# One core, a Perceiver layer with a top-2 mixture of experts: the first slot tiles in another order, and a gather that nobody reads

## What is computed

```python
x = x + xattn(layernorm(x), ctx_1024, ...)   # 16 heads, 257 keys per batch
x = x + mix(layernorm(x), WB, WBf, w1, w2, b)
x = x + moe(layernorm(x), gate, w0, w1, wo)

# moe, 8 experts, F = 512, TOPK = 2
weights, selected = top_k(inputs @ gate, 2)
weights = softmax(weights)
layer_1, layer_2 = sorted_hidden @ w0[e], sorted_hidden @ w1[e]
layer_3 = (silu(layer_1) * layer_2) @ wo[e]
out = sum over the two choices of weights * layer_3
```

## Time and profile before

| | |
|---|---|
| median of 3 runs | 232.37 us (231.4 to 232.68) |
| profiled execution, its own time | 230.8 us |
| its span (first to last instruction) | 229.0 us |
| mean granted TensorE clock | 0.984 of full |
| TensorE busy | 211.3 us, 92% of the span |
| VectorE, ScalarE, GpSimd busy | 66%, 62%, 57% |
| chain that ended last | TensorE 79%, DMA 6%, VectorE 6%, GpSimd 3%, "issue" 2% |

### The profile page before, as it was taken

The page is one execution under the profiler, slowest core; times in us unless marked ns, Lnnn a source line. Parts: engine busy times, 40 slices in busy tenths (PEclk is TensorE's granted clock), DMA queues, the critical chain, the costliest instruction groups (busy, mean ns, idle before and its releaser), DMA issues.

```text
span 229.0 us, 6348 instructions
## 1 busy us (share of the span) xinstructions
PE 211.3 (92%) x2123; PEld 176.6 (77%) x2123; DVE 150.3 (66%) x504; ACT 141.0 (62%) x440; POOL 129.9 (57%) x268
## 2 busy tenths in 40 slices
PE   6789999999999999999987887997999999999980
PEld 6567778778777776867864874796999999999870
DVE  2789769778686877858768587933445565555702
ACT  2488897888899888879875446651224444444300
POOL 2665474566647554561526733947777777773312
PEclk9999999999999999999999999799999999999996
DMA  6888134070411910000000004402212211121053
GB/s 182 291 280 306 63 67 168 0 232 0 161 74 27 337 54 3 1 4 0 4 3 0 1 3 116 71 3 47 58 49 46 58 40 51 45 35 35 2 186 93
DMA packets 12817, 18.30 MB, mean 80 GB/s; under 512 B 1903, under 2 KB 8435, under 8 KB 12786
## 3 DMA queue, kind: packets, MB, share of 16 engines
q1 hardware_dynamic: 10946, 14.77, 20.4%
q0 software_dynamic: 1408, 2.58, 5.1%
q10 hardware_dynamic: 432, 0.54, 0.7%
HBM read 14.20 MB, written 4.01 MB: 80 GB/s over the span
## 4 chain that ended last, share of the span: by engine, by line
PE 79%; DMA 6%; DVE 6%; POOL 3%; issue 2%; ACT 1%; POOLq 1%; SPq 0%; DVEq 0%
PE bank L1041 17%; PE bank L845 12%; PE bank L835 10%; PE bank L817 8%; PE bank L877 8%; PE bank L1052 8%; PE bank L819 6%; DMA pt_sb<-planes 2%; PE bank L1010 2%; PE bank L854 2%; DMA vec_sb<-vectors 2%; DMA slot_sb<-table,slot_row 1%; PE bank L1028 1%; DMA planes<-y_sb,y_row 1%; DVE neg_max L1201 1%
## 5 line engine op out<-in xcount | busy, mean ns | idle before, releaser
L669 ACT ACTIVATE p_sb<-bank,neg_max 128x257 f32<-128x257 f32 x128 | 59.1, 475 | 16.0 <-DVE neg_max L1201 16.0
L1201 DVE TENSOR_REDUCE neg_max<-bank 128x1 f32<-128x257 f32 x128 | 46.7, 418 | 6.4 <-PE bank L835 6.0
L678 ACT ACTIVATE pt_sb<-bank 128x512 f32<-128x512 f32 x64 | 35.0, 612 | 0.6 <-PE bank L845 0.6
L508 POOL TENSOR_TENSOR o_half<-o_masked 128x64 f32<-128x64 f32 x32 | 10.2, 320 | 44.1 <-DVE o_masked L1230 44.1
L845 PE MATMUL bank<-ident,p_sb 128*128 128x128 f32 x256 | 33.2, 273 | 0.0
L1041 PE MATMUL bank<-slot_ft,w_now 128*128 128x128 f32 x240 | 30.9, 276 | 0.0
L1041 PEld LDWEIGHTS bank<-slot_ft,w_now 128*128 128x128 f32 x240 | 29.1, 192 | 0.3 <-issue 0.3
L845 PEld LDWEIGHTS bank<-ident,p_sb 128*128 128x128 f32 x256 | 29.0, 141 | 0.3 <-issue 0.3
L745 ACT ACTIVATE slot_ft<-bank 128x128 f32<-128x128 f32 x23 | 6.4, 278 | 35.9 <-PE bank L1028 33.1
L567 POOL DMA_INDIRECT slot_sb<-table,slot_row x23 | 22.8, 991 | 9.6 <-issue 5.8
L587 POOL DMA_INDIRECT planes<-y_sb,y_row x21 | 21.5, 1023 | 11.4 <-DVE y_sb L1472 5.8
(11 more groups left out here) (212 smaller groups left out, 359.0 us busy)
## 6 DMA issues: line engine op xcount, KB each, us to landing
w_sb<-w SPq DMA_DIRECT2D x8, 512.0 KB, 4.8
ctx_sb<-ctx_keys SPq DMA_DIRECT2D x7, 512.0 KB, 4.3
wo_sb<-wo SPq DMA_DIRECT2D x8, 256.0 KB, 5.3
planes<-zero_rows SPq DMA_DIRECT2D x2, 512.0 KB, 6.8
pt_sb<-planes SPq DMA_DIRECT2D x4, 256.0 KB, 4.7
table<-rows_tok SPq DMA_DIRECT2D x4, 195.0 KB
out<-norm_tok SPq DMA_DIRECT2D x2, 256.0 KB, 2.4
x_tok<-x SPq DMA_DIRECT2D x1, 448.0 KB, 4.9
```

What stands on the lines that cost most here:

```text
L669: act.activation(p_sb[b % 2][:, g, :], s_bank[g][:, 0:SKV], ACT.Exp, bias=neg_max[b % 2][:, g:g + 1], accum_out=sum_last[:, 0, b, g:g + 1] ...
L678: act.activation(pt_sb[b % 2][:, t, :], pt_bank[t][:], ACT.Copy).then_inc((pt0_ready, pt1_ready)[t], 1)
L1201: dve.tensor_reduce(neg_max[b % 2][:, g:g + 1], s_bank[g][:, 0:SKV], AX.X, ALU.max, negate=True).then_inc(max_ready, 1)
```

## The change

It has six parts.

1. `keep_sum(1)` moves ahead of the ranks, behind `keep_sum(0)`.
2. Of tile 1's one-hots GpSimd makes one (token tile 0) in place of four; VectorE makes the other three in one instruction, behind `at_slot`. TensorE's products of tile 1 are put in the order token tile 0, tiles 4 to 7, tiles 1 to 3.
3. `name_slots` moves ahead of tile 1's product.
4. `turn_slots(s + 1)` for s = 1 and 2 moves ahead of `project(s - 1)`.
5. GpSimd issues one more indirect DMA ahead of its one-hots: 128 times row 2048 of the table into `slot_sb[5]`. Nobody reads it; its landing is waited for ahead of the real gathers.
6. For that, a column `no_row` that holds 2048, and a semaphore of its own for the storing of the empty row.

```diff
+        no_row = sb("no_row", [128, 1], U32)
...
-            sp.dma_start(table[TABLE_ROWS:TABLE_ROWS + 1, :], empty_row[0:1, :]).then_inc(table_stored, 16)
+            sp.dma_start(table[TABLE_ROWS:TABLE_ROWS + 1, :], empty_row[0:1, :]).then_inc(empty_stored, 16)
...
+                pool.iota(no_row[:], [[0, 1]], base=TABLE_ROWS, channel_multiplier=0).then_inc(consts_ready, 1)
...
+            pool.wait_ge(consts_ready, 13)
+            pool.wait_ge(empty_stored, 16)
+            pool.indirect_dma_start(slot_sb[SLOT_BUFS - 1][:], None, table, bass.IndirectOffsetOnAxis(no_row[:], 0)
+                                    ).then_inc(first_gather_in, 16)
+
             pool.wait_ge(early_rank_ready, 1)
             for s in range(EARLY):
-                for t in range(HT):
+                for t in range(HT if s == 0 else 1):
                     pool.tensor_scalar(late_at[s][:, t, :], far_slot_nos[:], early_rank[:, t, s:s + 1], None, ALU.is_equal
                                        ).then_inc(pool_at_ready[s], 1)
 
-            pool.wait_ge(table_stored, 16 * (TOPK * len(GROUPS) + 1))
+            pool.wait_ge(table_stored, 16 * TOPK * len(GROUPS))
             pool.wait_ge(slot_row_ready, 1)
+            pool.wait_ge(first_gather_in, 16)
             for s in (2, 0, 3, 1, 4, 5):
                 gather(s)
...
             keep_sum(0)
+            keep_sum(1)
             pe.wait_ge(chosen_ready, 1)
...
-            keep_sum(1)
...
+            def early_features_1():
+
+                pe.wait_ge(pool_at_ready[1], 1)
+                early_product(1, 0, True, False)
+                for t in range(HT):
+                    pe.wait_ge(act_at_ready[1], t + 1)
+                    early_product(1, HT + t, False, False)
+                pe.wait_ge(dve_at_ready, 1)
+                for t in range(1, HT):
+                    last = early_product(1, t, False, t == HT - 1)
+                last.then_inc(slot_turned, 1)
...
-            early_features(0)
+            early_features_0()
             half_hidden(0, 0)
             half_hidden(0, 1)
-            early_features(1)
             name_slots()
+            early_features_1()
...
                 half_hidden(s, 1)
+                if s <= EARLY:
+                    turn_slots(s + 1)
                 if s == 1:
                     pe.wait_ge(slot_row_ready, 1)
                 project(s - 1)
-                if s <= EARLY:
-                    turn_slots(s + 1)
...
+            few = [128, HT - 1, 128]
+            dve.tensor_tensor(late_at[1][:, 1:HT, :], far_slot_nos[:].unsqueeze(1).to_broadcast(few),
+                              early_rank[:, 1:HT, 1:2].to_broadcast(few), ALU.is_equal).then_inc(dve_at_ready, 1)
+
             dve.wait_ge(slot_row_done, 1)
```

More of the change, by code:

```diff
@@ L259, in build @@
             sem(n) for n in ("row_in_tile_ready", "at_slot_ready", "slot_row_done", "slot_row_ready"))
+        first_gather_in, empty_stored = sem("first_gather_in"), sem("empty_stored")
         early_rank_ready, apart_ready = (sem(n) for n in ("early_rank_ready", "apart_ready"))
         pool_at_ready, act_at_ready = ([sem(f"{name}{n}") for n in range(EARLY)] for name in ("pool_at_ready", "act_at_ready"))
+        dve_at_ready = sem("dve_at_ready")
         block = stack.enter_context(nc.Block())
@@ L752, in gate_weights @@
                                ACT.Copy).then_inc(gate_w_ready, 1)
-            act.wait_ge(consts_ready, 12)
+            act.wait_ge(consts_ready, 13)
             act.wait_ge(early_rank_ready, 1)
@@ L987, in _ @@
             keep_sum(0)
+            keep_sum(1)
             pe.wait_ge(chosen_ready, 1)
-            pe.wait_ge(consts_ready, 12)
+            pe.wait_ge(consts_ready, 13)
             for t in range(NT):
@@ L1000, in _, with early_product, early_features_0 @@
             last.then_inc(ranks_done, 1)
-            keep_sum(1)
[L1005 to L1011, removed]
+            def early_product(s, t, start, stop):
+                return pe.matmul((bank[3], bank[1])[s][:, 0:128], rows_tok[:, t, 0, 0:D], late_at[s][:, t, :],
+                                 start=start, stop=stop)
+            def early_features_0():
+                for t in range(HT):
+                    pe.wait_ge(pool_at_ready[0], t + 1)
+                    early_product(0, t, t == 0, False)
+                    pe.wait_ge(act_at_ready[0], t + 1)
+                    last = early_product(0, HT + t, False, t == HT - 1)
+                last.then_inc(slot_turned, 1)
+            def early_features_1():
+                pe.wait_ge(pool_at_ready[1], 1)
+                early_product(1, 0, True, False)
+                for t in range(HT):
+                    pe.wait_ge(act_at_ready[1], t + 1)
[3 more added lines that the diff above has]
+                    last = early_product(1, t, False, t == HT - 1)
                 last.then_inc(slot_turned, 1)
@@ L1359, in _ @@
             own(best_at(2))
-            dve.wait_ge(consts_ready, 12)
+            dve.wait_ge(consts_ready, 13)
             te = [128, NT, E]
```

## The result

| | before | changed |
|---|---|---|
| median | 232.4 us (231.4 to 232.68, 4 runs) | 228.28 us (227.94 to 229.48, 4 runs) |
| ratio | 1 | 0.9856, 95% interval 0.9817 to 0.9896 |
| profiled execution, own time | 230.8 us | 227.94 us |
| its span | 229.0 us | 226.1 us |
| mean granted TensorE clock | 0.984 | 0.997 |

The change is faster, by 1.0 to 1.8%. The forecast was 229.3 us, in a range from 227.6 to 231.2.

What follows compares the result with a forecast made beforehand. TensorE, busy 92% of the span, was taken as the bound, with time to win at its slow-clock slice and idle places from 143 to 163 us. 232.37 - 3.1 = 229.3 us; range 227.6 to 231.2.

Steps and rivals of the forecast that it cites:

- The walk along TensorE: TensorE's work followed from 143.35 us at the full clock through half_hidden(4); 3.1 us won in all.
- the signs: Expected in the profile after: earlier half_hidden(0) and slot_row, no idle before turns 2 and 3, clock not below 0.9.
- keep_sum(1), 0.97 us: Moved into TensorE's 0.95 us hole before the ranks at cost 0; half_hidden(0) starts at 147.15, 0.97 us won.
- name_slots and the turns: name_slots first gives slot_row at 149.87, not 152.63; turns ahead of projections start half_hidden(2) at 154.80, not 157.00.
- The spare gather: Extra GpSimd gather before the one-hots, 2.09 us within 3.44 us idle; cost 0, keeps gathers just ahead of TensorE.
- a lag of 0.30 or 0.84 us: First real gather starts 0.84 us after slot_row, or 0.30 if the spare gather takes the first one's extra.
- The bound of 0 to 0.9 us for a late slot 4: At turn 4: without the spare gather's help, slot 4 could hold TensorE by 0 to 0.9 us.
- The last step: From profiled execution to median: 3.1 us taken off 232.37 gives 229.3; the profiled execution was 1.57 us below the median.
- the clock falls elsewhere: Rival, chance 0.37: clock falls during or behind tile 0's product; gain 2.6 us (0.22) or 1.8 us (0.15).
- The gathers are late: Rival, chance 0.08: extra 0.84 us and long landings make turn 4 wait 0.9 us; gain 2.2 us, 230.2 us.
- The slower case: Rival, chance 0.05: spare gather holds GpSimd too long, delaying tile 0's one-hots; 234.2 us, or 234.6 us.

Runs made afterwards that it cites:

- e3: Changed kernel with keep_sum(1) behind the ranks again; ratio 0.9884 to the kernel before, chosen to half_hidden(4) 18.78 us.
- e11: Kernel before with only keep_sum(1) moved ahead of the ranks; ratio 1.0001 to the kernel before, chosen to half_hidden(4) 21.48 us.
- e4: Changed kernel with turns 2 and 3 behind the projections again; ratio 0.9905 to the kernel before, chosen to half_hidden(4) 19.36 us.
- e5: Changed kernel with name_slots behind tile 1's product again; ratio 0.9937 to the kernel before, chosen to half_hidden(4) 20.99 us.
- e2: Changed kernel without the spare gather; median 229.25 us, ratio 0.9889 to the kernel before, chosen to half_hidden(4) 18.34 us.
- e10: Changed kernel without the spare gather, run once more; median 228.75 us, ratio 0.9877 to the kernel before, chosen to half_hidden(4) 18.33 us.
- e1: Changed kernel run again unaltered; median 227.92 us, ratio 0.984 to the kernel before, chosen to half_hidden(4) 18.10 us.
- e9: Changed kernel run once more unaltered; median 228.57 us, ratio 0.9857 to the kernel before, chosen to half_hidden(4) 18.10 us.
- e7: Changed kernel with four spare gathers in place of one; ratio 1.0148 to the kernel before, chosen to half_hidden(4) 24.71 us.
- e6: Changed kernel with VectorE working out tile_expert behind the first hid_ft; ratio 0.9859 to the kernel before, chosen to half_hidden(4) 18.11 us.
- e12: Kernel before with only the spare gather added; ratio 0.9972 to the kernel before, chosen to half_hidden(4) 20.47 us.

## Why the prediction was right

The walk along TensorE was right in its order and its waits, and within 0.25 us in every step. I set it beside the trace. The measured times are those of the changed trace, which runs 0.14 us ahead of the other (`chosen` at 142.37 against 142.51), so counted from `chosen` every measured start is 0.14 us later than it reads here:

| step | foretold | measured |
|---|---|---|
| first one-hot on GpSimd | 143.67 | 143.53 |
| `half_hidden(0)` starts | 147.15 | 147.15 |
| VectorE's three one-hots | 0.6 us | 0.55 us |
| `slot_row` known | 149.87 | 149.81 |
| tile 1's product | 1.79 us | 1.90 us |
| `half_hidden(1)` starts | 151.75 | 151.84 |
| `half_hidden(2)` starts | 154.80 | 154.90 |
| `half_hidden(4)` starts | 160.37 | 160.48 |
| gain in the traces | 3.1 us | 2.9 us |

Counted so, the first one-hot came when foretold, `half_hidden(0)` 0.14 us late and `half_hidden(4)` 0.25 us late (18.11 us behind `chosen` against 17.86); the other 0.11 is tile 1's product. Of the signs, two did not come: the first real gather began 0.77 us behind `slot_row` where 0.3 was foretold, and the clock's last slice stands at 8 tenths (6 before), at the program's end. GpSimd's first one-hot, the turns without a wait and the clock behind 146.6 came as foretold.

**keep_sum(1), 0.97 us.** It did fit the hole: the ranks' first matmul follows `chosen` as closely as before. `half_hidden(0)` came 0.83 us earlier behind `chosen` (4.78 against 5.61). Its value is that of the clock. e3 gives 0.67 us inside the change. By itself, in e11, it gave nothing. Its worth can't be told apart from where the clock then falls.

**name_slots and the turns.** e4 gives 1.25 us for the turns, e5 about 1.6 for `name_slots` with the clock's share taken off. With e3's 0.67 that makes 3.5 us, more than the whole of 2.86, which fits parts that share one path: with the slots late anyway, an earlier turn is worth less. Part 2, the one-hots given to VectorE, was not run by itself. With the old split GpSimd's last one-hot of tile 1 ended at 150.58 (before) and 150.65 (e11), about 1 us behind the 149.59 at which the changed kernel starts that product.

**The spare gather.** Costing it at 0 was right in the stretch. I had left open a lag of 0.30 or 0.84 us behind it and read that the first might lose its extra. It lost 0.23 us of duration and 0.1 of lag. The bound of 0 to 0.9 us for a late slot 4 held: 0.22 (e2, e10). By the Trainium skill's GPSIMD Engine Reference (section Instruction dispatch) the first call of freshly loaded GpSimd code pays about 6 us; no trace here shows that, the first gather took 1.25 us wherever it stood.

**The last step,** from the trace to the median, is the least sure. I took 3.1 us off the median; the medians are 4.1 us apart in the result, and 4.0 and 3.0 in the groups of e1 and e9. The foretold 3.1 us is 1.3% and lies inside all three intervals of the ratio; the spans' 2.9 us is 1.25%, inside two of them and at the edge of e1's (1.24 to 1.97%). So these runs don't show the step wrong, and that the median landed within 1.0 us of the forecast is no proof of it. That the profiled execution of the kernel before stood 1.57 us below its median has the size by which heads (up to 1.5 us) and ends (up to 1.1 us) differ between traces; in its trace the head is of the early kind and the end, at 14.8 us, on the short side; that both were late in the median's execution is not shown, as only profiled executions have a trace. Whether in the other executions the order before loses more than in its trace, because the clock falls elsewhere there, stays open.

**The rivals.** That the clock falls elsewhere came true in e5 and e11, not in a trace of the changed kernel. The gathers are late by 0.22 us without the spare one. The slower case needed three more gathers (e7).

## What to carry to other kernels

When work moves off a path into an idle hole of TensorE, ask where the next hole opens, and price what stands behind it at half the clock: the same move was worth 0.67 us in one order and nothing in another, and e5 shows that the fall can come or stay away behind the same pause. Put the transpose that feeds a copy ahead of the matmuls that can cover the copy, and the work whose result travels through a DMA ahead of work whose result stays on the engine. Compare traces from a common event close to the change, as a program's start and end can each differ by a third to a half of what a change like this one is worth.

## What the runs showed of the hardware that was not expected

- A first real gather, for which GpSimd had long waited, began 0.75 to 0.90 us behind its release in all fourteen traces, and the next ones 0.30 us behind the one before. An earlier gather took 0.23 us off its duration (1.25 to 1.02) and 0.13 us off the lag (0.90 to 0.77).
- Near the start of the program the same matmuls took twice as long in four of fourteen traces, up to about 11 us, which moved everything behind by 1.1 to 1.5 us. In e9 and e10 the granted clock was 0.50 there; in e6 and e12 it was 1.00.
- The granted clock fell from 1.00 to 0.50 after a pause of TensorE of only 0.95 us and a run of matmuls with 8 columns (before). Behind a pause of 1.08 us it fell in two traces (e5, e11) and stayed at 1.00 in eight, the changed kernel's three among them, though e5's work up to there is the changed kernel's.
- GpSimd's one-hot of 0.60 us took 2.70 us beside `at_slot` on VectorE (before, e7, e11).
